# A fused attention and mixture-of-experts layer on one core: work of three passages moved, and a VectorE read-out put ahead of a clip

## The reference

```python
x = x + layernorm(attention(layernorm(x)))     # x: (8, 1024, 256) float32
x = x + layernorm(ffn(layernorm(x)))

# attention: 16 heads of 16 + 8 rotary dimensions, latent of 64
scores  = clip(Q K^T, -80, 80), causal
weights = softmax(scores / sqrt(24));  out = (weights V) W_O

# ffn on (8192, 256), 8 experts, top 2, two iterations
ctx = concat(integrated, v)
ctrl_shared = gelu(ctx @ shared_w1 + b) @ shared_w2 + b
ctrl_expert = gelu(ctx @ w1[e] + b1[e]) @ w2[e] + b2[e]     # the chosen e
a, b, g = split(ctrl, 3)
v_next = sigmoid(a) * v - softplus(b) * (x - mu)
x_next = x + 0.1 * sigmoid(g) * v_next
# shares, halting gate, twice; then
out = xf + integration_weight * (gelu(integrated @ refine_w1 + b) @ refine_w2 + b)
```

## Time and profile before

| | before |
|---|---|
| median of 3 runs | 2930.03 us |
| the profiled execution, its own time | 2933.28 us |
| its span, first to last instruction | 2931.6 us |
| mean granted TensorE clock | 0.936 |
| busy: TensorE, VectorE, ScalarE, GpSimd | 2591.9, 2269.5, 1933.7, 608.6 us |

### The profile page before, as it was taken

The page is one execution under the profiler, slowest core; times in us unless marked ns, Lnnn a source line. Parts: engine busy times, 40 slices in busy tenths (PEclk is TensorE's granted clock), DMA queues, the critical chain, the costliest instruction groups (busy, mean ns, idle before and its releaser), DMA issues. The chain is left out here.

```text
span 2931.6 us, 43059 instructions
## 1 busy us (share of the span) xinstructions
PE 2591.9 (88%) x16032; PEld 1799.7 (61%) x16032; DVE 2269.5 (77%) x3931; ACT 1933.7 (66%) x3075; POOL 608.6 (21%) x424
## 2 busy tenths in 40 slices
PE   3788888888888967899999999999999999997997
PEld 2233333333323313688888888788788888886897
DVE  4577777667676656789889998999989988886555
ACT  1676766667676844566667666666767766665786
POOL 2012031211112111111121121211111121210476
PEclk8899989999898967899999999999999999999999
DMA  3552525254351631000000000000000000000442
GB/s 101 87 86 61 91 65 92 75 90 79 67 101 52 93 90 51 1 1 15 15 1 15 15 15 8 8 16 15 15 1 15 15 15 8 1 8 27 147 133 73
DMA packets 125634, 136.75 MB, mean 47 GB/s; under 512 B 17410, under 2 KB 105474, under 8 KB 125428
## 3 DMA queue, kind: packets, MB, share of 16 engines
q1 hardware_dynamic: 125428, 134.00, 20.1%
HBM read 87.56 MB, written 46.40 MB: 46 GB/s over the span
## 5 line engine op out<-in xcount | busy, mean ns | idle before, releaser
L491 ACT ACTIVATE probs<-psum_a 128x1024 f32<-128x1024 f32 (+3 forms) x768 | 601.1, 815 | 333.9 <-PE psum_a L807 329.6
L1487 PE MATMUL psum_f<-w,picked 128*128 128x256 f32 (+1 forms) x2304 | 712.3, 342 | 0.0
L1486 PE MATMUL psum_f<-w,picked 128*128 128x256 f32 x2304 | 617.4, 285 | 1.2 <-DVE picked L1306 1.2
L1487 PEld LDWEIGHTS psum_f<-w,picked 128*128 128x128 f32 x2304 | 444.5, 193 | 51.5
L567 DVE TENSOR_SCALAR probs<-probs 128x2048 f32<-128x2048 f32 (+3 forms) x320 | 304.0, 950 | 203.6 <-ACT probs L491 203.6
L807 PE MATMUL psum_a<-q_stack,k_stack 72*128 72x512 f16 (+3 forms) x1536 | 396.3, 349 | 56.3 <-ACT probs L491 35.0
L1486 PEld LDWEIGHTS psum_f<-w,picked 128*128 128x128 f32 x2304 | 445.1, 193 | 1.5 <-DVE picked L1306 1.5
L822 PE MATMUL psum_a<-probs,v 128*17 128x512 f32 (+3 forms) x3072 | 342.8, 520 | 10.6 <-DVE attn L579 5.9
L807 PEld LDWEIGHTS psum_a<-q_stack,k_stack 72*128 72x128 f16 x1536 | 100.6, 101 | 400.8 <-ACT probs L491 238.7
L1306 DVE TENSOR_TENSOR picked<-hid,masks 128x512 fp32r<-128x512 f32 x512 | 335.0, 714 | 10.0 <-PE psum_f L1487 6.8
L1127 ACT ACTIVATE gates<-psum_f 128x256 f32<-128x256 f32 (+1 forms) x384 | 186.4, 487 | 233.1 <-PE psum_f L1487 231.3
(11 more groups left out here) (289 smaller groups left out, 5408.2 us busy)
## 6 DMA issues: line engine op xcount, KB each, us to landing
heads_scratch<-kq_parts SPq DMA_DIRECT2D x64, 256.0 KB
k_stack<-heads_scratch SPq DMA_DIRECT2D x96, 128.0 KB
q_stack<-heads_scratch SPq DMA_DIRECT2D x96, 128.0 KB
x_in<-x_dram SPq DMA_DIRECT2D x8, 1024.0 KB, 5.5
x_res<-x_dram SPq DMA_DIRECT2D x16, 512.0 KB, 4.8
x_scratch<-y SPq DMA_DIRECT2D x16, 512.0 KB, 3.1
xs<-x_scratch SPq DMA_DIRECT2D x16, 512.0 KB, 3.9
xf_scratch<-xs SPq DMA_DIRECT2D x16, 512.0 KB, 2.9
```

The lines of the kernel that those rows point to most:

```text
L491: act.activation(probs[:, s % PROB_SETS, 2 * u:2 * u + 2, q0:512], psum[:, 2 * u:2 * u + 2, q0:512], ACT.Exp, scale=exp_scale).then_inc(ex ...
L1486: pe.matmul(soft_out, x, cols[:, 1], start=start, stop=stop)
L1487: return pe.matmul(gate_out, x, cols[:, 2] if it == 0 else cols[:, 0::2], start=start, stop=stop)
```

## The change

1. In attention VectorE's read-out of the job of tick T-2 stands at the head of tick T, ahead of the clip of tick T-1.
2. The late loads go from the end of SP's window 6 to window 7, behind the second residual load. The product with mu becomes a job of attention (`MU`, ticks 36 to 41 of window 7, 12 matmuls on unsplit weights), the splits go to ticks 37 to 46, the last two of the first layer's wait for that job.
3. Block 0 of the mixture is loaded, its statistics taken (last tick) and normalized (three ticks on) within attention, into `xs[:, 0]`, which lies over the value buffer of even batches. The rows of the very last half go to a buffer `y_last` there too, so ScalarE's last two copies don't wait for a store.
4. The mixture starts with the transposes of block 0. The clearing and the constant rows come after block 0's `x_lower`. Block 1 is loaded after the last store, blocks 2 and 3 at once.
5. The refinement's weights are loaded into the first layer's place once the last hidden job is done, split in the last four units (`split_refine`), and multiplied with mu after the last slot. Blocks 0 and 1 for it are loaded then too. There is no wait for the last store at the block's end.

```diff
+    MEAN_TICK = (BATCH - 1) * STEPS + 36
+    MEAN_COLS = 6
+    job_at[MEAN_TICK + MEAN_COLS - 1] = ("MU", BATCH - 1, 0, 0)
+    SPLIT_TICK = MEAN_TICK + 1
+    X_FIRST_TICK = ALL_STEPS - 1
...
+                if w == BATCH - 1:
+                    sp.wait_ge(late_cleared, 1)
+                    for dst, src in late_loads:
+                        sp.dma_start(dst, src).then_inc(late_in, 16)
+                    sp.wait_ge(pv_done, STEPS * w)
+                    sp.dma_start(late.x_first[:], x1_dram.rearrange("(i t p) d -> i p t d", p=P, t=BT)[0]).then_inc(x_first_in, 16)
...
+                    if (b, half) == (BATCH - 1, 1):
+                        act.wait_ge(pv_done, STEPS * b)
+                    elif (b, half) != (0, 0):
                         act.wait_ge(x1_stored, 16 * (2 * b + half))
-                    dst = y[:, 2 * i:2 * i + 2, :]
...
+            def first_stats():
+
+                dve.wait_ge(x_first_in, 16)
+                for t in range(BT):
+                    last = dve.bn_stats(x_stats[:, t, :], late.x_first[:, t, :])
+                then_wait(last)
+                spread_of(x_stats[:, 0:BT], BT, late.row_scale[:, 0, 0], x_veps[:, 0:BT]).then_inc(x_first_stats, 1)
+
+            def first_normalize():
+
+                x = late.x_first
+                dve.wait_ge(x_first_rstd, 1)
+                for t in range(BT):
+                    last = dve.tensor_scalar(x[:, t, :], x[:, t, :], late.row_scale[:, 0, 0, t:t + 1], late.row_scale[:, 1, 0, t:t + 1],
+                                             ALU.subtract, ALU.mult)
+                then_wait(last)
+                dve.tensor_tensor(x[:], late.mu[:].unsqueeze(1).to_broadcast([P, BT, D]), x[:], ALU.subtract).then_inc(late.x_first_ready, 1)
+
             for tick in TICKS:
                 w, t = tick // STEPS, tick % STEPS
+                if tick - 2 in job_at and job_at[tick - 2][0] in ON_DVE:
+                    read_out(job_at[tick - 2])
                 if 0 <= tick - 1 < ALL_STEPS:
                     clip(tick - 1)
-                if w == BATCH - 1 and 24 <= t < 24 + late.SPLITS:
-                    split_late(t - 24)
+                if tick == X_FIRST_TICK:
+                    first_stats()
+                if tick == X_FIRST_TICK + 3:
+                    first_normalize()
+                if SPLIT_TICK <= tick < SPLIT_TICK + late.SPLITS:
+                    split_late(tick - SPLIT_TICK)
                 for gci in range(ALL_ACCS):
                     if last_tick(gci) + PV_LAG + 3 == tick:
...
+            def mean_column(m):
+
+                job = ("MU", BATCH - 1, 0, 0)
+                bank = psum[:, WORK_BANK + number[job] % 2, :]
+                if m == 0:
+                    pe.wait_ge(late_in, 16 * len(late_loads))
+                    bank_free(job)
+                for c in range(2):
+                    w = late.raw_w1[:, 1, c, P * m:P * m + P] if m < 5 else late.raw_wr1[:, 1, c]
+                    last = pe.matmul(bank[0:w.shape[1], m:m + 1], w, late.mu_col[:, c:c + 1], start=(c == 0), stop=(c == 1))
+                if m == MEAN_COLS - 1:
+                    last.then_inc(job_done, 1)
...
-            sp.wait_ge(late.x1_stored, 16 * XS)
-            for k in range(XS):
+            for k in (2, 3, 1):
+                if k == 1:
+                    sp.wait_ge(late.x1_stored, 16 * BLOCKS)
                 sp.dma_start(xs[:, k], blk_v[k]).then_inc(x_loaded[k], 16)
-            sp.wait_ge(late.x1_stored, 16 * BLOCKS)
             for k in range(BLOCKS):
+                if k == BLOCKS - 1:
+                    job_ready(sp, ("H", k, 1, FULL - 1))
+                    for dst, src in refine_loads:
+                        sp.dma_start(dst, src).then_inc(late.f_in, 16)
+                    n = first_unit[k - 1, 1] + BT - 1
+                    sp.wait_ge(upper_picked, 2 * n + 2)
+                    sp.wait_ge(lower_picked, 2 * n + 2)
+                    for q in range(2):
+                        sp.dma_start(late.xf[:, q], xf_v[q]).then_inc(late.xf_loaded[q], 16)
                 sp.wait_ge(unit_done, first_unit[k, 1] + BT)
                 sp.dma_start(xf_v[k], xs[:, k % XS]).then_inc(xf_stored[k % XS], 16)
                 if k + XS < BLOCKS:
                     sp.wait_ge(xf_stored[k % XS], 16 * (k // XS + 1))
                     sp.dma_start(xs[:, k % XS], blk_v[k + XS]).then_inc(x_loaded[k % XS], 16)
...
-            x_row_stats(0)
-            first_values()
-            x_normalize(0)
...
+            def split_refine(step):
+
+
+                wf1, wf2, raw_f1, raw_f2 = late.wf1, late.wf2, late.raw_f1, late.raw_f2
+                if step == 0:
+                    dve.wait_ge(late.f_in, 16 * len(refine_loads))
+                    for m in range(MC):
+                        dve.tensor_tensor(raw_f2[:, 1, m], raw_f2[:, 1, m], late.iw[:], ALU.mult)
+                    dve.tensor_tensor(late.bf2[:], late.bf2[:], late.iw[:], ALU.mult)
+                    last = dve.tensor_copy(wf1[:, 0], raw_f1[:, 1])
+                else:
+                    dve.wait_ge(late.f_split, step)
+                if step == 1:
+                    dve.tensor_copy(wf2[:, 0], raw_f2[:, 1])
+                    last = dve.tensor_tensor(wf1[:, 1], raw_f1[:, 1], wf1[:, 0].bitcast(F32), ALU.subtract)
+                if step == 2:
+                    last = dve.tensor_tensor(wf2[:, 1], raw_f2[:, 1], wf2[:, 0].bitcast(F32), ALU.subtract)
+                if step == 3:
+                    dve.scalar_tensor_tensor(out=late.shift[:], in0=mean, scalar=-1.0, in1=rstd, op0=ALU.mult, op1=ALU.mult)
+                    dve.wait_ge(late.f_mean, 1)
+                    last = dve.tensor_tensor(late.bf1[:], late.bf1[:], psum[:, 0, 0:MC], ALU.add)
+                last.then_inc(late.f_split, 1)
+
...
+            for job in jobs[-3:]:
+                bank_read(pe, job)
+            pe.wait_ge(late.f_split, 2)
+            for m in range(MC):
+                for c in range(2):
+                    for part in range(2):
+                        last = pe.matmul(psum[:, 0, m:m + 1], late.wf1[:, part, c, P * m:P * m + P].bitcast(F32), mu_col[:, c:c + 1],
+                                         start=(c == 0 and part == 0), stop=(c == 1 and part == 1))
...
```

More of the change, by code:

```diff
@@ L406, in add_residual @@
                 pool.wait_ge(y_ready, n)
-                pool.tensor_tensor(y[:], y[:], x_res[:], ALU.add).then_inc(sum_ready, 1)
+                rows = y_of(b, half)
+                pool.tensor_tensor(rows[:], rows[:], x_res[:], ALU.add).then_inc(sum_ready, 1)
             def x_scale(b):
@@ L641, in y_row_stats @@
                 for t in (2 * i, 2 * i + 1):
-                    last = dve.bn_stats(y_stats[:, t, :], y[:, t, :])
+                    last = dve.bn_stats(y_stats[:, t, :], y_of(b, half)[:, t, :])
                 if i == 1:
@@ L711, in _ @@
                         divide(gci)
-                if tick - 2 in job_at and job_at[tick - 2][0] in ON_DVE:
-                    read_out(job_at[tick - 2])
                 if 0 <= w - 1 < BATCH:
@@ L843, in _, with mixture @@
                         turn(gci)
-                if tick in job_at:
+                if MEAN_TICK <= tick < MEAN_TICK + MEAN_COLS:
+                    mean_column(tick - MEAN_TICK)
+                elif tick in job_at:
                     run(job_at[tick])
-def mixture(nc, late, x1_dram, xf_dram, row_scale):
+def mixture(nc, late, x1_dram, w_dram, xf_dram):
     blk_v = x1_dram.rearrange("(i t p) d -> i p t d", p=P, t=BT)
@@ L977, in mixture @@
         x_loaded = [sem(f"f_x_loaded{q}") for q in range(XS)]
-        mu_part = sem("f_mu_part")
-        xf_stored = [sem(f"f_xf_stored{q}") for q in range(XS)]
+        xf_stored = late.xf_stored
+        refine_loads = late.refine_loads(w_dram)
         stats_ready = sem("f_stats_ready")
@@ L1404, in _ @@
             pe.wait_ge(late.split, late.SPLITS)
-            for m in range(6):
-                for c in range(2):
-                    for part in range(2):
-                        w = w1[:, part, c, P * m:P * m + P] if m < 5 else wr1[:, part, c]
-                        last = pe.matmul(psum[0:w.shape[1], 0, m:m + 1], w.bitcast(F32), mu_col[:, c:c + 1],
-                                         start=(c == 0 and part == 0), stop=(c == 1 and part == 1))
-            last.then_inc(mu_part, 1)
-            pe.wait_ge(weights_ready, 1)
             def bank_free(job):
@@ L1525, in refine @@
     BLOCKS = TOKENS // BLOCK
-    mean, rstd = row_scale[:, 0], row_scale[:, 1]
+    mean, rstd = late.row_scale[:, 0], late.row_scale[:, 1]
     BUFS, AHEAD = 6, 4
@@ L1610, in _ @@
         def _(sp):
-            for dst, src in loads:
-                sp.dma_start(dst, src).then_inc(weights_in, 16)
             def load_xf(k):
+                sp.wait_ge(late.xf_stored[k % 4], 16 * (k // 4 + 1))
                 sp.dma_start(xf[:, k % AHEAD], xf_v[k]).then_inc(xf_loaded[k % AHEAD], 16)
@@ L1783, in _ @@
         def _(pe):
```

(10 more changed lines are left out.)

173 lines of the change are left out of this document (92 added, 81 removed).

## The result

The changed kernel takes **2781.2 us** in the median (2780.7 to 2782.1, four runs), the kernel before beside it 2928.1 (2920.3 to 2935.5): ratio **0.949** [0.948, 0.951], 147 us less. Forecast: 2778. The profiled execution took 2781.4 us, span 2779.7, mean granted clock 0.955 (before 2933.3, 2931.6, 0.936): 151.9 us less.

A forecast was written before the change was run, and what follows sets the result against it. The prediction saw attention held by TensorE's waits for VectorE's late read-outs, with low clock, a window 7 stall and two passages adding time. 2933.3 with -88 -23 -19 +3 -13.6 -14.7 gave 2778 us, own range 2755 to 2805.

The forecast's parts named there:

- A: Attention windows 0 to 6: read-outs ahead of clips remove most of TensorE's waits, 13.5 of 15.6 us in six windows; -88 us.
- clock: Windows 0 to 6: some low-clock stretches of TensorE go with the waits; -23 us, bounds 0 and -55.
- B: Window 7 of attention: late loads moved behind the residual, so ScalarE's stall goes; -19 us.
- C: End of attention: splits at ticks 37 to 46 cost +0.7, first block's statistics +2.3; +3 us, bounds 0 and +8.
- the forecast's sign, that waits for clips stay under 3 us: Attention windows: if the forecast holds, TensorE's waits for clips stay under 3 us.
- Tail and first passage: Attention's end to the mixture: own row buffer, transposes at block start, x_res as new last wait; -13.6 us, bounds -17 and -8.
- E: Mixture to refinement: weights loaded and split in the last four units; transposes -15.7, cold start +1; -14.7 us.
- The mixture's steady units are untouched: Mixture between the passages: its steady units, 1491 us, don't change.
- R1: Rival, attention: only the waits go and the clock stays as it is; 2801 us, chance 0.2.
- R3: Rival, attention windows: clips put back by read-outs hold TensorE, the three-tick lag not hiding them; 3022 us, chance 0.02.
- R2: Rival, attention windows: VectorE becomes the bound, half of the waits' and clock's gains stay; 2834 us, chance 0.15.
- R4: Rival, window 7: the stall only moves, late loads holding TensorE after tick 36; 2788 us, chance 0.05.

The follow-up runs named there:

- experiment 8: Changed kernel with the normalization of attention's output rows one tick later: 2782.2 us, ratio 0.9487 to the kernel before.
- experiment 12: Changed kernel with one extra VectorE instruction (128x512, result unused) behind each read-out of windows 0 to 6: 2852.9 us, ratio 0.9717.
- experiment 2: Changed kernel with VectorE's read-out put back behind the clip and the division: 2900.6 us, ratio 0.9893 to the kernel before.
- experiment 1: Kernel before with only VectorE's read-out of a job moved ahead of the clip of its tick: 2820.6 us, ratio 0.9615.
- experiment 3: Kernel before with 288 unused bytes ahead of soft_b, putting the mixture's working tiles at the changed kernel's addresses: 2948.1 us, ratio 1.0041.
- experiment 6: Changed kernel with 224 unused bytes ahead of soft_b, restoring the working tiles' old remainder by 512: 2771.9 us, ratio 0.9453.
- experiment 4: Kernel before with only the late loads moved behind window 7's second residual and the splits moved to ticks 37 to 46: 2910.9 us, ratio 0.9918.
- experiment 10: Experiment 6 with 22 late loads ahead of window 7's first store, mean job at ticks 27 to 32, splits every second tick from 28: 2769.0 us, 0.9434.
- experiment 11: Experiment 6 with the last half's residual loaded early into a place of its own: 2765.1 us, ratio 0.9422.
- experiment 7: Changed kernel with 40 late loads ahead of window 7's first store, mean job 13 ticks sooner, splits at every second tick: 2790.0 us, ratio 0.9515.

## Why the prediction was right, and where only in sum

- **A and clock: right as a sum, and partly luck, as one term was too large and the other too small.** Forecast -111 for windows 0 to 6, measured -112.8 and, alone, -115.1; the four traces with the old order take 915.5 to 918.1 us there, eight with the new one 800.5 to 804.9 (experiments 8 and 12 change the queue besides). But per window the waits gave 10.1 us (15.6 to 5.5), not 13.5, and 7.2 of the 17.3 come from elsewhere. The clock fits: at 0.92 a window of 133.1 us loses 10.6 us of full speed, at 0.96 to 0.97 one of 116.5 loses 3.5 to 4.7. That is 6 to 7 less, where 3.5 were forecast. The waits that were left are mostly those at ticks 11 to 15, which the step named, but at 3.6 us where it left 1.3: the instructions in front of them are longer beside GpSimd's sums. No run separates wait and clock, so this split is read from rows, not shown by an experiment. The Trainium skill (TensorE: Matmul & The Clock Gate, "What's actually happening") says that activity releases the throttle; the forecast made -50 of that for this term. By these rows it is some -40 over the windows, nearer to that than to the -23 chosen.
- **Window 7: the step that was missed.** A was counted for windows 0 to 6 only. Window 7 reads out the last output jobs as well, and experiment 2 against the full change puts the order's part there at 6.5 us; as long as the stall stood (experiment 1) it gave only 1.7.
- **B and C: nearly right in sum (-19.5 measured alone, -18.3 forecast without the statistics), less so in their parts.** The stall's stretch gave 21.8 us, not 19. The loads took 31.7 us, where some 30 were forecast, and TensorE didn't stand for them. Moving the splits cost 2.3 us, not 0.7: 13.4 us went from ticks 24 to 35, and 9.0 came in ticks 36 to 47 and 6.7 behind the last exponential. VectorE works there almost without a gap, 27.5 of 28.9 us. Behind the last exponential it does splits ahead of the last clips, and TensorE's matmuls wait 5.9 us for these (rows below, changed kernel); in the kernel before there is no such wait of a matmul, and one of 0.6 us of a weight load. So the forecast's sign, that waits for clips stay under 3 us, held in the windows, not here.

```profile
991.50 0.84 PE L916 MATMUL psum_a<-probs,v 128*17 128x384 f32 x8 [2.16 <-DVE probs L618]
...
995.37 1.06 PE L916 MATMUL psum_a<-probs,v 128*17 128x256 f32 x8 [3.04 <-DVE probs L618]
...
998.17 0.63 PE L916 MATMUL psum_a<-probs,v 128*17 128x128 f32 x8 [0.70 <-DVE probs L614]
```

- **Tail and first passage.** ScalarE's wait went, GpSimd waited 2.8 us for x_res, which landed 4.8 us behind its issue: the new last wait was named rightly. The passage gave 9.0 in place of 11.8; over all traces the old form took 43.6 to 45.0 us (four) and the new one 31.2 to 34.6 (nine others and the changed kernel), in the means 10.6 apart, so 9.0 is at the low end.
- **E: right**, -15.4 and +0.4 for -15.7 and +1; the transposes came 1.0 us behind the last update (within 1.5 forecast).
- **"The mixture's steady units are untouched": wrong**, +10.1 us. They run the same instructions, and the units became slower (8.34 to 8.41 us where TensorE is never late). Experiments 3 and 6 show the cause, the tiles' addresses: with the change shid, picked and their neighbours lie 288 bytes further on. Some 5 of the 10 us are that rate, the rest is time at the low clock. This goes with the addresses as well (29.2 to 40.1 us lost in the six traces with slots 8.34 apart, 40.7 to 44.2 in the six with 8.41), but no run shows how. That this loss and what window 7 gave beyond its forecast (7.7 us) nearly cancel in the total is luck.
- **Rivals.** R1 (clock stays) is excluded by the rise from 0.92 to 0.96 and more. R3 (clips' lag not hidden) didn't happen in the windows: waits for clips are 2.5 us, all at weight loads. R2 is the closest of them: VectorE isn't the bound at 97 of 116 us, but experiment 12 finds half of its added work in the window's length. R4: no wait at the mean job.

## What to carry to other kernels

In an engine's ordered list, put the work that another engine is waiting for ahead of the work that itself waits for a third engine. Count the gain for every stretch that has such pairs, the last one too. After an edit that allocates anything ahead of the operands of a stage bound by TensorE, compare the distance of two identical matmuls in an undisturbed stretch; if it moved, pad the allocation back (here to the old remainder by 512). A mean busy share of 83% isn't slack: the margin has to be measured where the queue is gapless.

## What the runs showed of the hardware

- The rate of the same matmul stream depends on where its tiles lie in SBUF: with picked at byte 184288 8.34 us for a unit of 24 pairs, at 184576 8.41, at 184608 8.39 to 8.40, at 184800 8.34; the mixture follows with 1492, 1502, 1512 and 1494 us, a part of which is the clock (34, 41, 51 and 37 us of full speed lost). The six kernels with picked at the old remainder by 512 and its neighbours moved alike (before, experiments 1, 4, 6, 10, 11) all showed 8.34 and mixtures of 1488 to 1496 us, the six at 184576 (changed, experiments 2, 3, 7, 8, 12) all 8.41 and 1502 to 1505. A single matmul's duration hardly shows it (0.28 to 0.29 and 0.39 to 0.40 us); only the distance over a unit does.
- Late-load issues behind the reloads of the stacks: 43.5 us for all of them before the change, 31.7 in the changed kernel at a calmer time. In experiment 7 the first 40 took 36 us.
- A GpSimd sum of the residual took 2.34 us alone, 6.0 and 6.3 in window 7 of the changed kernel, and VectorE's clip of 128x512 beside one 2.53 us in place of 0.68.
